# A two-stream transformer block on one core: the loop over units written out, and one order of steps per engine for the whole run

## The reference

```python
h = layernorm(x) * (1 + ca) + sa              # adaptive modulation from a small matrix c
x = x + ga * trajectories(h, guides)          # "new": differences of neighbours, a softmax over 64 guides,
                                              # and a weighted sum over a band of 8 positions
h = layernorm(x) * (1 + cb) + sb
for l in range(2):                            # two layers
    q, k, v = split(shift_token(h) @ wqkv[l]) # 8 heads of 64
    q, k = rotary(l2norm(q) * qs, l2norm(k) * ks)
    h = h + local_attention(q, k, v, window=64) @ wo[l]
    a, g = split(layernorm(shift_token(h)) @ w1[l] + b1[l])
    h = h + (a * gelu(g)) @ w2[l] + b2[l]
x = x + gb * h
```

## Time and profile before

| | |
|---|---|
| three runs | 999.84, 1001.75, 1000.94 us, median 1000.94 |
| profiled execution | 999.81 us, of which the span of the trace is 998.0 |
| PE busy | 794.4 us (80%), weight loads 563.6 |
| DVE, ACT, POOL busy | 674.9 (68%), 652.6 (65%), 568.1 (57%) |
| mean granted TensorE clock | 0.93 |
| DMA | 10 GB/s on average |

### The profile page before, as it was taken

How to read it: one execution, slowest core, us unless ns; L and a number is a source line. 1 busy time by engine, 2 the same in 40 slices (tenths; PEclk the granted TensorE clock), 3 DMA queues, 4 the chain that set the end, 5 groups by cost and what they waited for, 6 DMA issues and landing times.

```text
span 998.0 us, 19976 instructions
## 1 busy us (share of the span) xinstructions
PE 794.4 (80%) x7119; PEld 563.6 (56%) x7151; DVE 674.9 (68%) x1588; ACT 652.6 (65%) x1539; POOL 568.1 (57%) x324
## 2 busy tenths in 40 slices
PE   4355886979789797888889797888889887979875
PEld 3233664656566565565566565665566555656553
DVE  4565875675896874584897776575896765766542
ACT  0242765767676775676786876676786766868662
POOL 2046754483963762393984773393983763675600
PEclk9766799999989998999999999999999998999996
DMA  6000000000000000000000000000000000000000
GB/s 199 0 1 0 11 2 12 1 2 2 1 2 2 22 2 25 1 2 1 2 2 1 23 2 22 2 2 1 2 1 6 7 2 11 1 2 2 2 1 21
DMA packets 12286, 9.95 MB, mean 10 GB/s; under 512 B 1040, under 2 KB 11288, under 8 KB 12184
## 3 DMA queue, kind: packets, MB, share of 16 engines
q1 hardware_dynamic: 12184, 8.64, 2.9%
HBM read 6.54 MB, written 2.10 MB: 9 GB/s over the span
## 4 chain that ended last, share of the span: by engine, by line
PE 37%; DVE 18%; issue 17%; ACT 15%; POOL 12%; DMA 1%; SPq 0%; ACTq 0%; DVEq 0%; POOLq 0%
PE pair L439 7%; ACT probs L714 7%; PE dense L576 4%; PE mixed L470 3%; POOL qk L1246 3%; PE dense L539 3%; POOL root L1206 3%; POOL h_lo L1222 3%; DVE q_norm L1150 3%; DVE space L1145 3%; PE dense L541 3%; PE dense L540 3%; PE dense L654 2%; DVE neg_max L964 2%; DVE space L1143 2%
## 5 line engine op out<-in xcount | busy, mean ns | idle before, releaser
L1246 POOL TENSOR_TENSOR qk<-space 128x512 f32<-128x512 f32 x128 | 197.4, 1555 | 33.7 <-DVE q_norm L1150 29.1
L1206 POOL TENSOR_TENSOR root<-power,minus_half 128x32 f32<-128x32 f32 x32 | 173.8, 5432 | 0.0
L714 ACT ACTIVATE probs<-pair,neg_max 128x128 f32<-128x128 f32 x512 | 138.6, 387 | 20.6 <-DVE neg_max L964 20.3
L1145 DVE TENSOR_TENSOR space<-dense,tables 128x512 f32<-128x512 f32 x128 | 87.3, 682 | 57.6 <-ACT space L836 54.5
L654 PE MATMUL dense<-wq_hi,h_hi 128*128 128x512 f32 x192 | 94.4, 491 | 23.7 <-POOL h_lo L1235 12.4
L832 ACT ACTIVATE squares<-dense 128x512 f32<-128x512 f32 x128 | 77.4, 605 | 40.0 <-PE dense L656 39.0
L1243 POOL TENSOR_TENSOR space<-space,tables 128x512 f32<-128x512 f32 x64 | 86.1, 1346 | 27.9 <-ACT space L836 27.9
L964 DVE TENSOR_REDUCE neg_max<-pair 128x4 f32<-128x512 f32 x128 | 82.0, 682 | 25.9 <-PE pair L502 25.9
L439 PE MATMUL pair<-eye_s,probs 128*128 128x128 f32 x512 | 79.3, 289 | 25.1 <-ACT probs L714 25.1
L1235 POOL TENSOR_TENSOR h_lo<-shifted,h_hi 128x512 fp32r<-128x512 f32 x16 | 20.2, 1265 | 129.3 <-DVE h_hi L1132 129.3
L944 DVE TENSOR_TENSOR qk<-qk,root 128x2048 f32<-128x2048 f32 x32 | 83.8, 2618 | 4.4 <-POOL root L1206 4.4
(11 more groups left out here) (164 smaller groups left out, 1867.6 us busy)
## 6 DMA issues: line engine op xcount, KB each, us to landing
x_in<-n_L_attn_embeddings_dram SPq DMA_DIRECT2D x8, 256.0 KB, 3.3
out_dram<-hn SPq DMA_DIRECT2D x8, 256.0 KB, 2.4
qk<-in_L_ffn_wqkv_dram SPq DMA_DIRECT2D x1, 1536.0 KB, 6.3
qk<-in_L_ffn_w_dram SPq DMA_DIRECT2D x1, 682.0 KB, 7.7
wo_s<-in_L_ffn_wo_dram SPq DMA_DIRECT2D x2, 256.0 KB
o_t<-in_L_wmod_dram SPq DMA_DIRECT2D x1, 384.0 KB, 3.3
probs<-const_rotary_dram SPq DMA_DIRECT2D x1, 256.0 KB, 3.6
band_s<-const_band_dram SPq DMA_DIRECT2D x1, 256.0 KB, 7.9
```

Source lines behind the costliest of these rows:

```text
L714: last = act.activation(probs[:, ring, hh, :], banks[m][:, hh * P:(hh + 1) * P], ACT.Exp, bias=neg_max[:, ring, hh:hh + 1], scale=1.0)
L1145: dve.tensor_tensor(turned_s[:, t % 2, m, :].rearrange("p (h a b) -> p h a b", h=HEADS, a=2), halves[:, :, ::-1, :], rot(layer, t, 2 * m + 1),
L1206: return pool.tensor_tensor(to, of, minus_half[:, 0:of.shape[-1]], ALU.pow)
L1246: pool.tensor_tensor(qk[s][:, t, m * INNER:(m + 1) * INNER], turned_c[:, t % 2, m, :], turned_s[:, t % 2, m, :], ALU.add).then_inc(added, 1)
```

## The change

The loop is gone: all turns from -1 to 4 are written out, and with it go the register arithmetic for waits and addresses, the branch, and the four waits between turn 0 and the loop. `ORDER` now holds one list per engine and turn, six lists each. A step may stand among those of another slot: `>` means that a step of the next turn stands in this list, `<` one of the turn before. The ring of three banks follows PE's new order. Three kinds of wait are added, so that the shared halves stay right in any order: DVE's `ff.hi` and `proj.split` wait for the last product that read the halves in their previous use (`wait_halves_free`), ACT's `proj.split` for POOL's last read of `shifted`, and PE's `ff.up` and `proj.tile` for their halves at each step instead of at the first one. The arithmetic is unchanged.

```diff
+        found.append((turn, int(slot), tuple(int(part) if part.isdigit() else part for part in name.split("."))))
...
-    "pe": [*2 * [steps("""
-        a.turn.0 a.turn.1 ff.stats a.score.0 a.score.1 a.flip.0 a.mix.0 ff.norm a.out.0 a.flip.1 ff.up.0
...
+        3:a.mix.2 3:a.flip.3 3:a.out.2 3:a.mix.3 >0:a.turn.0 3:a.out.3 3:ff.norm 3:new.mix 3:proj.tile.3.1
+        3:proj.tile.3.2 3:a.project 3:new.sum 3:ff.up.0 3:ff.up.1 >0:a.turn.1 >0:a.score.0 3:ff.up.2
+        3:ff.down 3:new.stream"""),
...
-        def every_turn(eng, name, take, after_first=None):
-
-            def turn(i):
-                for slot in range(4):
-                    for step in ORDER[name][slot]:
-                        if runs(i, slot, step, turns):
-                            take(i, slot, step)
-            turn(-1)
-            turn(0)
-            if after_first:
-                after_first()
-            with eng.Fori(1, turns - 1) as i:
-                turn(i)
-            turn(turns - 1)
-            turn(turns)
+        def every_turn(eng, name, take):
+
+            for i in range(-1, turns + 1):
+                for turn, slot, step in ORDER[name][i + 1]:
+                    take(i + turn, slot, step)
...
+        halves_in_turn = [(i, slot, kind) for i in range(turns + 1) for slot in range(4)
+                          for kind in ((FF, PROJ) if slot < 2 else (PROJ, FF)) if runs(i, slot, (kind,), turns)]
+
+        def wait_halves_free(eng, i, slot, kind):
+
+            at = halves_in_turn.index((i, slot, kind))
+            if at:
+                last, its_slot, which = halves_in_turn[at - 1]
+                step, n = ((FF, "up", 2), 1) if which == FF else ((PROJ, "tile", TILES - 1, 2), 0)
+                eng.wait_ge(*filled_at(last, its_slot, step, n))
...
-                    if step[2] == 0:
-                        pe.wait_ge(ff_lo, before + 1)
+                    pe.wait_ge(ff_lo, before + 1)
...
+                    if past(before):
+                        act.wait_ge(qkv_lo, before)
                     shift((y_t if slot < 2 else y_new)[s], qkv_shifted)
...
                 elif what == "hi":
-                    if slot > 1 and runs(i, slot, (PROJ, "split"), turns):
-
-                        dve.wait_ge(*filled_at(i, slot, (PROJ, "tile", TILES - 1, 2)))
+                    wait_halves_free(dve, i, slot, FF)
```

More of the change, by code:

```diff
@@ L109, in runs @@
 def runs(i, slot, step, turns):
-    return not isinstance(i, int) or 0 <= unit_of(i, slot, step[0]) < turns
+    return 0 <= unit_of(i, slot, step[0]) < turns
 class BankTurns:
     def __init__(self, turns):
-        self.turns = turns
-        self.bank = {}
+        self.place = {}
         place = 0
-        self.steps = []
-        for slot in range(4):
-            for step in ORDER["pe"][slot]:
+        for i in range(-1, turns + 1):
+            for turn, slot, step in ORDER["pe"][i + 1]:
                 for n in range(BANKS_OF.get(step[:2], 0) if step[0] != "a" else 0):
-                    self.bank[(slot, step, n)] = place % DENSE_BANKS
-                    self.steps.append((slot, step, n))
+                    self.place[(i + turn, slot, step, n)] = (place % DENSE_BANKS, place // DENSE_BANKS)
                     place += 1
-    def before(self, i, key):
-        count = 0
-        for other in self.steps:
-            if other == key:
-                break
-            if self.bank[other] == self.bank[key] and runs(i, other[0], other[1], self.turns):
-                count += 1
-        return count
-    def whole(self, i, bank):
-        return sum(self.bank[k] == bank and runs(i, k[0], k[1], self.turns) for k in self.steps)
-    def of(self, i, slot, step, n=0):
-        key = (slot, step, n)
-        bank = self.bank[key]
-        full = self.whole(None, bank)
-        if isinstance(i, int):
-            return bank, sum(self.whole(j, bank) for j in range(-1, i)) + self.before(i, key)
-        return bank, i * full + (self.whole(-1, bank) + self.whole(0, bank) - full + self.before(None, key))
+    def of(self, i, slot, step, n=0):
+        return self.place[(i, slot, step, n)]
 def past(count):
-    return not isinstance(count, int) or count > 0
+    return count > 0
 def adaln_block(nc, x, traj, wqkv, q_scale, k_scale, wo, ln_g, ln_b, w1, b1, w2, b2, c, wmod,
@@ L423, in _ @@
             turn(0, False)
-            with sp.Fori(1, turns - 1) as i:
+            for i in range(1, turns - 1):
                 turn(i, False)
@@ L756, in feed_forward @@
                     src = bank(i, slot, step, 0)
-                    if chunk == 0 and slot > 1 and runs(i, slot, (PROJ, "split"), turns):
+                    if slot > 1 and runs(i, slot, (PROJ, "split"), turns):
                         act.wait_ge(added, 8 * (proj(i, slot)[1] + 1))
@@ L1166, in take @@
                     new_unit(i, slot, step)
-                    if isinstance(i, int) and i < 0 and step[1] in ("turn", "weights"):
+                    if i < 0 and step[1] in ("turn", "weights"):
                         finish_setup(("turn", "weights").index(step[1]))
```

398 lines of the change are left out of this document (334 added, 64 removed).

## The result

The changed kernel takes 967.0 us (median of 4 runs, 966.65 to 969.07) where the kernel before, run beside it, took 1001.35 (999.84 to 1003.6): ratio 0.9659, 95% interval [0.9636, 0.9683]. The time lies within the range of 925 to 987 and within the forecast's own 942 to 968, at its upper edge: 34 us were gained where 46 were summed. The profiled execution has a span of 965.0 us.

A forecast was written before the change was run, and what follows sets the result against it. Bound by neither one engine nor one wait, but by how well two dependent streams fill each other's gaps. Seven terms sum to -46 us: 999.8 - 46 = 953.8, 954 us; forecast 942 to 968, range for 8 times in 10 925 to 987.

The forecast's parts named there:

- Cold start: Turn 0: the other stream's unit starts 9.1 us earlier on PE; between 0 and -9.1 us, taken as -7.
- The wait for the input: Slot 3 of turns 1 and 2: DVE's `new.stats` no longer waits for the load; 0 to twice -3.3 us, taken -5.
- The branch back: After `store.turn`, where the loop jumps back once: PE's stop goes when written out; -3.4 to -5.6 us, taken -5.
- The borders: Six slot borders, 2 to 3 and 3 to 0: early attention steps fill PE's idle time; -3 us each, -18 together.
- The halves beside the scaling: Slots 0 and 1: POOL's eight long subtractions no longer run beside `a.unit`; 0 to -2.0 us each, -8 together.
- the rule on the shared port: Skill text: VectorE instructions with at most one SBUF input don't contend with GpSimd; would give -16 instead of -8, 946 us.
- The end: Last feed-forward goes ahead of `a.project`, so addition and last `ff.stats` come earlier; -3 to -8.6 us, taken -7.
- `new.dots` ahead of the lone attention: Turns 1 and 3: `new.dots` holds two of three banks, so the second tile waits; 0 to +12 us, taken +4.
- rival (A): Only stops with a plain cause go; borders and halves give nothing, as what is filled is missing later; 982 us, chance 0.22.
- (C): Slower: at six borders a late step holds up feed-forward, store and next `ff.stats`; 1014 us, chance 0.08.
- (B): Borders fill completely and halves reach their end, -36 and -16 us, and idle holding the clock down goes; 928 us, chance 0.21.

The follow-up runs named there:

- the old order with the one move: The written-out program with every engine's steps in the order before, but DVE's `a.unit` behind `ff.up.0` in slots 0 and 1: 967.9 us, ratio 0.9663.
- the one move: DVE's `a.unit` put behind `ff.up.0` in slots 0 and 1; alone, in the kernel before with its loop: 979.8 us, ratio 0.9779.
- the new order's best form: The kernel of 947.9 us with turn 2's slot 3 and the slot 0 behind it written as in turn 1: 942.2 us, ratio 0.9397.
- the run with the move undone: The changed kernel with `a.unit` directly behind `ff.hi` again in slots 0 and 1 of turns 1 to 4: 991.7 us, ratio 0.9904.

## Why the prediction was right, and where its terms were wrong

The time lies in the range mostly by luck. Terms 1, 2, 4, 6 and 7, the new order proper, were to bring 33 us of the 46; the old order with the one move takes 967.9 and the changed kernel 967.0, so on the whole they brought nothing. Terms 3 and 5, the branch and the halves, were to bring 13; the old order written out with the move is 34 us below the kernel before. By its terms:

1. Cold start, -7: failed. The step that failed is "between 0 and -9.1; I take -7": the unit reached PE 6.4 us earlier and the split that needs it came no earlier. In both looks at the changed kernel some 3 us went to the clock. In the one look without that loss the unit reached PE at 56.87, as the prediction asked, and the split stood at 98.99, against 99.8, 100.3 and 100.6 in three looks at the old start written out. That is about 1 us of 7. Between the unit's start and the split 8 us were lost again, most likely where the chain met the tiles, as the text feared; no run separates it.
2. The wait for the input, -5: the wait is gone (543.77, no DMA), the gain hardly there. In the old order with the move it is still there, 2.3 us twice, and its slot 3 takes 58.5 against 57.3 in the new order's best form. All changes of this stretch together are 1.2 each.
3. The branch back, -5: right, 5.9, or 4.8 with the move. The written-out old order with the move has 23.8 and 23.8 where the loop with the move has 28.6 and 23.9.
4. The borders, -18: half right. The idle time behind them fell as forecast, by 3.5 and 4.0 at one pair. Into slot 0 it stayed won: 4.0, 1.7 and 2.9 us against the old order with the move, and another 6 from turn 0 to 1, which the term had not counted. Into slot 3 it did not. The stretches to slots 2 and 3 have to be taken together, since `ff.down` stands later: 150.9 and 146.2 us in turns 1 and 2, against 142.5 both times in the old order with the move. Even the best form (86.8 + 57.3) is 1.6 longer; only in turn 3, where no new unit follows, is it 7.3 shorter (87.0 + 44.6 against 84.0 + 54.9). "The work stays the same, so a border can give" holds at the border; the step that failed is to add it up without asking what the lists give up for it elsewhere. With the old lists in slots 1 and 2, the new start, borders and end together are worth 20 and 26 us (967.9 to 947.9 and 942.2); in the changed kernel its own lists of slots 1 and 2 take all of it back.
5. The halves beside the scaling, -8: far too small, and the one that carries most. The move alone is worth 22 us in the kernel before and 18.6 in the old order written out, 2.2 to 2.3 in each inner slot. In the changed kernel six of the eight halves are short, and PE's wait for them fell from 31.4 to 9.8 us; its share of the time is not shown alone there, as the run with the move undone mixes it with waits for the scaling. The row with 3.61 us of PE's idle showed a place with nothing beside it. I discounted the 2.0 us by half for waits that would come in its place; with the move alone none came, in the new order two halves stayed long. The end of the range, -16, which the rule on the shared port gave, was the right reading, and still low.
6. The end, -7: the mechanism right, the gain smaller. Behind the last addition 7.2 us went (29.7 to 22.5, from the last L956 and L1207 to the last store's addition), but ahead of it, from the last `proj.split` on, 3.8 came back (61.9 to 65.7), most likely since the feed-forward's 7 us of PE did not fit into gaps. Left are some 3. Against the old order written out it is 2.0 with the new last turn alone (90.1 to 88.0 from that split to that store), and the timed run has 4 together with slots 0 and 1 of that turn, whose halves give 4.3 in the profile.
7. `new.dots` ahead of the lone attention, +4: right in place, 7.3 when the form of these two slots is taken away.
8. Not in the list: the collision of `xn`, 4 us in turn 1. It is chance, as it also came up in turn 2 of the kernel before, for 2.1 us.

The number of rival (A), 982, is out, since the halves do give. But its reason, that what is filled at a border is missing later, held for the new order as a whole. (C) holds for none of the borders into slot 0. What (B) said of the halves was right.
